# Expert stage: half-width products held in PSUM, head pairs and candidate sums added on GpSimd

## The chip, the cores and the metric

One core of one Trainium2 chip. The metric is the device time of one launch in microseconds, the median of several runs.

## What is computed

The reference passes 16 x 512 rows of 256 numbers through six stages. Stages 1 and 3 are the same expert feed-forward (the change is in these two alone); the others are a dilated attention, two channel mixes and an attention across the batch. The expert part, cut:

```python
q = einsum('btd,ed->bte', h, W_q)                 # 4 heads, two halves each
sx, ix = top_k(sim[0], 8); sy, iy = top_k(sim[1], 8)
all_scores = sx[..., :, None] + sy[..., None, :]   # 64 candidates a head
scores, pk = top_k(all_scores, 8)
indices = take_along_axis(ix * 64 + iy, pk)        # clamped to 1024 experts by the lookup
w = silu(einsum(h, down_embed[indices]) * softmax(scores))
out = dense_mlp(h) + einsum(w, up_embed[indices])
```

## The kernel before

`expert_ffn` works on 256 rows a step: V = 2 tiles (v = 0, 1) of 128 rows. Each of its two stages has 32 steps, unrolled by four. It gathers nothing. For every row it computes the products of h with all 1024 experts (`dots`, into the two banks of `p_dot`), and for each of 4 heads a grid of all 1024 scores (GpSimd, `scores`, one 128x1024 addition a head). ScalarE turns the grid into exponentials (`exps`). VectorE finds the eighth best score of each head and makes the dense weights in two passes a head: `mask` (L648) writes (grid >= threshold) * p_dot to `q` in SBUF, `weigh` (L658) multiplies it in place by 1/z and by the grid. ScalarE applies silu to the whole of `q[v]` (128x4096, L536) and adds the share of the experts beyond 1023 to the last column (`tail`, `clamped`). TensorE transposes `q` in 128x128 blocks and sums the four heads as it does (`turn_w`, L436: 16 matmuls against the identity a call, 4 calls a step), ScalarE copies the transposed weights out (`turned`, L525), and TensorE multiplies them by `eup` (`experts`, L452) on top of the dense part (`dense`, L447).

The thresholds come from VectorE: `sides` takes the 8 best of each side by 12 MAX8 instructions, adds all pairs of them (`cand`, L604), takes the best of those by 8 MAX8 (L610, L611) and negates the best one (`negm`, L616). `listed` (VectorE) subtracts the maximum (`tm`, L621), `listed` (ScalarE) takes the exponential of it (`te`, L511), and `tails` (VectorE) makes z, 1/z (`rz`) and the share of the clamped experts (L627 to L636).

Every engine has its own instruction queue in a fixed order, written out in one function `step(t)` each; engines wait for each other by semaphores (`Track.mark`, `Track.wait`). In step t, VectorE selects for t and finds thresholds for t + 1, GpSimd makes the grids of t + 1, and TensorE finishes tile 1 of t - 1, then tile 0 of t. `p_dot` is single: `dots` for the next tile waits for the last mask of the tile before (mark "tail" of `d_mask`). Two instructions on one engine that depend on each other wait on a semaphore too. PSUM has 8 banks, all used: `p_dot` 2, `p_wT` 2, `p_sim`, `p_hid`, `p_y` 2. `norm.scale` (L195, called by `normed`), `front` (L174, L178) and `root` (GpSimd, L185, L187) are the layer norm of later steps.

Of the kernel before, what the change touches and what calls it, by code (L numbers as in the profile page):

```python
# [219 lines left out]
def expert_ffn(nc, name, src, dst, w):  # L220

    with ExitStack() as ctx:
# [62 lines left out]
        tops, tm, te = (m.sbuf(k, V, HEADS, 2 * TOP) for k in ("tops", "tm", "te"))  # L285
# [19 lines left out]
        d_top = m.track("d_top", *(f"{k}{v}" for v in range(V) for k in ("maxes", "cand", "best", "negm")), "tm")  # L305
        a_te = m.track("a_te")
        d_tail = m.track("d_tail", "z", "seen", "rz", "part", "tail")
        g_grid = m.track("g_grid", "0", "1")
        a_exp = m.track("a_exp", "0", "1")
        t_dot = m.track("t_dot", "0", "1")  # L310
        d_mask = m.track("d_mask", *(f"{v}{k}" for v in range(V) for k in (*range(HEADS), "tail")))
        d_mul = m.track("d_mul", "0", "1")
        a_silu = m.track("a_silu", *(f"{k}{v}" for v in range(V) for k in ("q", "tail", "clamped")))
# [11 lines left out]
        with nc.Block() as block:  # L325
# [25 lines left out]
            def _(pool):  # L351
                def scores(t, v):
                    a_sim.wait(pool, t, str(v))
                    if (t - 1).exists():
                        d_mul.wait(pool, t - 1, str(v))
                    sx = sim[:, v, 0:HEADS * KEYS].rearrange("p (h k) -> p h k", h=HEADS)[:, :, 0:XROWS]
                    sy = sim[:, v, HEADS * KEYS:].rearrange("p (h k) -> p h k", h=HEADS)
                    for hd in range(HEADS):
                        last = pool.tensor_tensor(  # L359
                            grid[v][:, hd, :].rearrange("p (i j) -> p i j", i=XROWS),  # L360
                            sx[:, hd, :].unsqueeze(2).to_broadcast([P, XROWS, KEYS]),
                            sy[:, hd, :].unsqueeze(1).to_broadcast([P, XROWS, KEYS]), ALU.add)
                    g_grid.mark(last, str(v))
# [3 lines left out]
                scores(first, 0)  # L367
                scores(first, 1)
                norm.root(pool, first + 2)

                def step(t):
                    if (t + 1).exists(last=count):
                        scores(t + 1, 0)
                        scores(t + 1, 1)
                    if (t + 3).exists(last=count):
                        norm.root(pool, t + 3)
                turns(pool, count, unroll, step)

            @block.tensor
            def _(pe):  # L380
# [47 lines left out]
                def turn_w(t, v, k):  # L428
                    a_silu.wait(pe, t, f"clamped{v}" if k else f"q{v}")
                    if v:  # L430
                        a_wT.wait(pe, t, f"0{k}")
                    elif (t - 1).exists():
                        a_wT.wait(pe, t - 1, f"1{k}")
                    for e in range(HALF):
                        for hd in range(HEADS):
                            last = pe.matmul(p_wT[k][:, e, :], q[v][:, hd, (k * HALF + e) * P:(k * HALF + e + 1) * P],  # L436
                                             ident[:], is_transpose=True, start=hd == 0, stop=hd == HEADS - 1)
                    t_wT.mark(last, f"{v}{k}")

                def dense(t, v):  # L440

                    if v == 0:
                        a_hid.wait(pe, t, "3")
                    if (t - 1).exists():
                        d_out.wait(pe, t - 1, str(v))
                    for e in range(EC):
                        pe.matmul(p_y[v][:], hs[t.step % 2][:, e, v * P:(v + 1) * P], wdn[:, e, :], start=e == 0, stop=False)  # L447

                def experts(t, v):
                    a_wT.wait(pe, t, f"{v}1")  # L450
                    for e in range(EC):
                        last = pe.matmul(p_y[v][:], wT[v][:, e, :], eup[:, e, :], start=False, stop=e == EC - 1)  # L452
                    t_out.mark(last, str(v))
# [1423 lines left out]
```

How the kernel before makes its waits and increments, by code:

```python
    def wait(self, engine, turn, name=None, alone=False):  # L59
        at = self.marks.index(name) + 1 if name else len(self.marks)
        n = len(self.marks) * self.inc
        engine.wait_ge(self.sem, turn.times(n, at * self.inc))
        if alone:
            engine.nop(nofuse=True)
# [59 lines left out]
    def sync(self, sp):  # L125
        sp.wait_ge(self.s_zero, self.STAGES)
        for n, (src, hi, lo, heads) in enumerate(self.loads):
            if n >= self.STAGES:
                sp.wait_ge(self.s_lo, n - self.STAGES + 1)
            raw = self.raw(n)
            if heads:
                raw = raw.rearrange("p (h s) -> p h s", s=heads[1])[:, :, 0:heads[0]]
                src = src.rearrange("p (h d) -> p h d", d=heads[0])
            sp.dma_start(raw, src).then_inc(self.s_ld[n % self.STAGES], 16)
# [1 line left out]
    def scalar(self, act):  # L136
        for n, (src, hi, lo, heads) in enumerate(self.loads):
            act.wait_ge(self.s_ld[n % self.STAGES], 16 * (n // self.STAGES + 1))
            act.copy(hi, self.raw(n)).then_inc(self.s_hi, 1)
# [1 line left out]
    def vector(self, dve):  # L141
        for k in range(self.STAGES):
            dve.memset(self.stage[k][:], 0.0).then_inc(self.s_zero, 1)
        for n, (src, hi, lo, heads) in enumerate(self.loads):
            dve.wait_ge(self.s_ld[n % self.STAGES], 16 * (n // self.STAGES + 1))
            dve.wait_ge(self.s_hi, n + 1)
            dve.tensor_tensor(lo, self.raw(n), hi.bitcast(F32), ALU.subtract).then_inc(self.s_lo, 1)
```

## Time and profile before

| | us |
|---|---|
| median of 3 runs | 4485.29 |
| lowest, highest | 4482.9, 4485.95 |
| the profiled execution | 4483.73 |
| its span, from first to last instruction | 4481.9 |
| first expert stage, in the span | about 20 to 1205 |
| second expert stage | about 2436 to 3623 |

In the page the busy shares are PE 91%, VectorE 80%, ScalarE 62%, GpSimd 30%. Busy shares are an average over six stages, so what matters here are views of the expert stages alone. Start-to-start times of instructions on one engine are shorter than their durations, because the end of one overlaps the start of the next.

### The profile page before, as it was taken

Reading aid. Unit: us, or ns where it says so; the run is one execution under the profiler, and the core shown is the slowest. Engines: PE = TensorE matmul, PEld = TensorE weight load, DVE = VectorE, ACT = ScalarE, POOL = GpSimd, SP = SyncE. Lnnn points to the kernel's source line nnn. Section 1 sums busy time; section 2 is a strip of 40 time slices with the busy share of each in tenths; the row PEclk is TensorE's granted clock in tenths of the full one; section 3 lists DMA queues with packets and bytes.
Section 4 is the critical chain, followed back from the end, with each engine's and each line's share of the span. In section 5 each row is a group of like instructions: output and inputs, shape, how many; then the busy total and the mean of one; then the engine's idle time right before and its main releaser. Section 6 shows DMA issues by size and latency. Waiting matters only on the chain. (4 is left out here: it accounts for less than half of the span.)

```text
span 4481.9 us, 87959 instructions
## 1 busy us (share of the span) xinstructions
PE 4096.4 (91%) x31208; PEld 3540.6 (79%) x31208; DVE 3574.9 (80%) x7869; ACT 2769.0 (62%) x6709; POOL 1331.1 (30%) x914
## 2 busy tenths in 40 slices
PE   6999999999779999999995999999999979787879
PEld 5988888888667777777774888888888867686756
DVE  7999999999657777777775999999999958445667
ACT  4777767667468887888883776766777723221123
POOL 3544444444221111111101444444444401011200
PEclk9999999999889999999997999999999989898989
DMA  1000000000100000000001000000000012358332
GB/s 59 15 16 15 16 15 15 15 19 14 33 17 11 21 11 21 12 21 21 12 11 64 10 15 16 16 15 20 16 16 15 10 60 89 140 196 246 104 96 76
DMA packets 175295, 180.47 MB, mean 40 GB/s; under 512 B 9552, under 2 KB 167536, under 8 KB 174832
## 3 DMA queue, kind: packets, MB, share of 16 engines
q1 hardware_dynamic: 174832, 174.40, 12.4%
q8 instruction: 278, 4.55, 0.4%
q14 instruction: 185, 1.52, 0.1%
HBM read 98.87 MB, written 75.50 MB: 39 GB/s over the span
## 5 line engine op out<-in xcount | busy, mean ns | idle before, releaser
L359 POOL TENSOR_TENSOR f_grid<-f_sim 128x1024 f32<-128x1024 f32 x512 | 1023.4, 2028 | 1182.2 <-DVE f_q L658 1174.0
L1277 ACT ACTIVATE a_ex<-a_p_s,a_mneg 128x128 f32<-128x128 f32 x2048 | 718.5, 403 | 211.4 <-DVE a_mneg L1322 211.4
L648 DVE SCALAR_TENSOR_TENSOR f_q<-f_grid,f_te,f_p_dot 128x1024 f32<-128x1024 f32 x512 | 620.8, 1273 | 133.4 <-ACT f_grid L517 101.0
L658 DVE SCALAR_TENSOR_TENSOR f_q<-f_q,f_rz,f_grid 128x1024 f32<-128x1024 f32 x512 | 622.5, 1276 | 0.0
L517 ACT ACTIVATE f_grid<-f_grid,f_negm 128x1024 f32<-128x1024 f32 x512 | 545.5, 1138 | 0.0
L1277 ACT ACTIVATION_READ_ACCUMULATOR a_ex<-a_p_s,a_mneg 128x1 f32 x2048 | 498.0, 243 | 0.0
L436 PE MATMUL f_p_wT<-f_ident,f_q 128*128 128x128 f32 x4096 | 480.1, 273 | 4.2 <-ACT f_q L536 4.1
L536 ACT ACTIVATE f_q<-f_q 128x4096 f32<-128x4096 f32 x128 | 464.4, 3628 | 20.9 <-DVE f_q L658 20.0
L436 PEld LDWEIGHTS f_p_wT<-f_ident,f_q 128*128 128x128 f32 x4096 | 457.4, 141 | 20.0 <-ACT f_q L536 4.5
L447 PE MATMUL f_p_y<-f_wdn,f_hs 128*128 128x256 f32 x2048 | 462.8, 379 | 1.4 <-ACT f_hs L531 1.4
L452 PE MATMUL f_p_y<-f_eup,f_wT 128*128 128x256 f32 x2048 | 462.8, 379 | 0.0
L447 PEld LDWEIGHTS f_p_y<-f_wdn,f_hs 128*128 128x128 f32 x2048 | 383.4, 190 | 54.0 <-ACT f_hs L531 1.8
L452 PEld LDWEIGHTS f_p_y<-f_eup,f_wT 128*128 128x128 f32 x2048 | 384.1, 190 | 49.9
L1328 DVE COPY a_exT<-a_p_s 128x512 f32<-128x512 f32 x384 | 264.7, 690 | 181.1 <-PE a_p_s L1147 174.8
L525 ACT COPY f_wT<-f_p_wT 128x512 f32<-128x512 f32 x256 | 143.0, 583 | 370.7 <-PE f_p_wT L436 370.7
L1322 DVE TENSOR_REDUCE a_mneg<-a_p_s 128x4 f32<-128x512 f32 x512 | 343.4, 671 | 11.5 <-PE a_p_s L1136 9.0
L531 ACT ACTIVATE f_hs<-f_p_hid 128x512 f32<-128x512 f32 x256 | 152.2, 594 | 252.2 <-PE f_p_hid L106 252.2
L1147 PE MATMUL a_p_s<-a_ident,a_ex 128*128 128x128 f32 x1536 | 244.7, 282 | 37.4 <-ACT a_ex L1277 37.2
L1147 PEld LDWEIGHTS a_p_s<-a_ident,a_ex 128*128 128x128 f32 x1536 | 166.5, 141 | 102.9 <-ACT a_ex L1277 86.3
L1061 POOL TENSOR_TENSOR a_xb<-a_xt,a_bos 128x256 f32<-128x256 f32 x64 | 44.8, 732 | 490.2 <-DVE a_yt L1360 488.8
L1136 PE MATMUL a_p_s<-a_kT,a_qz 32*128 32x128 f32 x4096 | 151.6, 284 | 37.0 <-DVE a_exT L1328 19.8
L1136 PEld LDWEIGHTS a_p_s<-a_kT,a_qz 32*128 32x128 f32 x4096 | 128.2, 187 | 55.6 <-issue 36.8
(368 smaller groups left out, 9486.6 us busy)
## 6 DMA issues: line engine op xcount, KB each, us to landing
x_f<-f_yt SPq DMA_DIRECT2D x64, 256.0 KB, 2.2
f_xt<-x SPq DMA_DIRECT2D x32, 256.0 KB, 2.8
a_xt<-x_f SPq DMA_DIRECT2D x16, 512.0 KB, 4.2
x_a<-a_yt SPq DMA_DIRECT2D x16, 512.0 KB, 2.9
f_xt<-x_a SPq DMA_DIRECT2D x32, 256.0 KB, 2.8
c_xt<-x_f SPq DMA_DIRECT2D x16, 512.0 KB, 4.6
x_c<-c_yt SPq DMA_DIRECT2D x16, 512.0 KB, 3.1
b1p_xt<-x_c SPq DMA_DIRECT2D x16, 512.0 KB, 4.2
```

What stands on the lines that cost most here:

```text
L359: last = pool.tensor_tensor(grid[v][:, hd, :].rearrange("p (i j) -> p i j", i=XROWS), sx[:, hd, :].unsqueeze(2).to_broadcast([P, XROWS, KE ...
L436: last = pe.matmul(p_wT[k][:, e, :], q[v][:, hd, (k * HALF + e) * P:(k * HALF + e + 1) * P], ident[:], is_transpose=True, start=hd == 0, s ...
L447: pe.matmul(p_y[v][:], hs[t.step % 2][:, e, v * P:(v + 1) * P], wdn[:, e, :], start=e == 0, stop=False)
L452: last = pe.matmul(p_y[v][:], wT[v][:, e, :], eup[:, e, :], start=False, stop=e == EC - 1)
L517: last = act.activation(grid[v][:, hd, :], grid[v][:, hd, :], ACT.Exp, bias=negm[:, v, hd:hd + 1])
L536: a_silu.mark(act.activation(q[v][:], q[v][:], ACT.Silu), f"q{v}")
L648: d_mask.mark(dve.scalar_tensor_tensor(out=q[v][:, hd, :], in0=grid[v][:, hd, :], scalar=te[:, v, hd, TOP - 1:TOP], in1=p_dot[:], op0=ALU. ...
L658: last = dve.scalar_tensor_tensor(out=q[v][:, hd, :], in0=q[v][:, hd, :], scalar=rz[:, v, hd:hd + 1], in1=grid[v][:, hd, :], op0=ALU.mult, ...
L1136: mm = pe.matmul(p_s[i][:, 2 * c + e, :], qz[br][lanes, c, e, j * P:(j + 1) * P], kT[br][lanes, c, j * P:(j + 1) * P], start=True, stop=True)
L1147: last = pe.transpose(p_e[i][:, n, :], ex[t.step % 2][:, i, n, :], ident[:])
L1277: last = act.activation(ex[t.step % 2][:, i, n, :], p_s[i][:, n, :], ACT.Exp, bias=mneg[:, i, n:n + 1], accum_out=z[t.step % 2][:, i, n:n ...
L1322: d_max.mark(dve.tensor_reduce(mneg[:, i, :], p_s[i][:], AX.X, ALU.max, negate=True), str(i))
```

## The change

- Two PSUM banks, `p_u[0]` and `p_u[1]`, hold the masked products. `mask` and `weigh` are cut in halves of 512 experts: 8 + 8 instructions of 128x512 for each tile in place of 4 + 4 of 128x1024. For each head there are two masks to PSUM, then two weighs from PSUM and the grid to `q`.
- The banks come from `p_wT` (one in place of two) and `p_y` (both tiles in one bank), which adds waits: every `turn_w` waits for the copy of the one before, `dense(t, 1)` for `output(t, 0)`, `dense(t, 0)` for `output(t - 1, 1)`.
- GpSimd gets the candidate sums (`pairs`, 128x512), two additions of head pairs for each tile (`summed`, 128x1024, q0 + q1 and q2 + q3 after silu), and a product for the clamped experts (`tails`). `turn_w` then transposes two sums in place of four heads: 8 matmuls a call.
- The grid, its exponentials, mask and weigh are marked and awaited by head. Silu works on two halves of two heads.
- `tm` is gone; ScalarE takes `te` by 8 activations of 128x16 with `negm` as bias. VectorE's five tail instructions become z, rz and 8 small `tensor_scalar` (`seen`).
- The orders on VectorE, GpSimd, ScalarE and TensorE are rewritten: on VectorE the output, `seen`, `maxes`, `best` and `normed` stand between the heads of `select`; on TensorE `dots(t, 1)` stands after `dense(t - 1, 1)` and half of `experts`.

```diff
-        p_wT = [m.psum(f"p_wT{k}", HALF, P) for k in range(2)]
-        p_sim, p_hid = m.psum("p_sim", 512), m.psum("p_hid", 512)
-        p_y = [m.psum(f"p_y{v}", D) for v in range(V)]
+        p_u = [m.psum(f"p_u{e}", 512) for e in range(2)]
+        p_wT, p_sim, p_hid = m.psum("p_wT", HALF, P), m.psum("p_sim", 512), m.psum("p_hid", 512)
+        p_y = m.psum("p_y", V, D)
...
+                def pairs(t, v):
+                    d_top.wait(pool, t, f"maxes{v}")
+                    g_cand.mark(pool.tensor_tensor(cand[:, v]..., tx[:, v]..., ty[:, v]..., ALU.add), str(v))
...
+                def summed(t, v, k):
+                    a_silu.wait(pool, t, f"clamped{v}" if k else f"front{v}")
+                    g_pair.mark(pool.tensor_tensor(q[v][:, 2 * k, :], q[v][:, 2 * k, :], q[v][:, 2 * k + 1, :], ALU.add),
+                                f"{v}{k}")
...
                 def step(t):      # GpSimd
-                    if (t + 1).exists(last=count):
-                        scores(t + 1, 0)
-                        scores(t + 1, 1)
-                    if (t + 3).exists(last=count):
-                        norm.root(pool, t + 3)
+                    tails(t)
+                    if after:
+                        pairs(t + 1, 0)
+                        scores(t + 1, 0, (0, 1))
+                    summed(t, 0, 0)
+                    summed(t, 0, 1)
+                    if after:
+                        pairs(t + 1, 1)
+                        scores(t + 1, 0, (2, 3))
+                    summed(t, 1, 0)
+                    if after:
+                        scores(t + 1, 1, (0,))
+                    summed(t, 1, 1)
+                    if (t + 3).exists(last=count):
+                        norm.root(pool, t + 3)
+                    if after:
+                        scores(t + 1, 1, (1, 2, 3))
...
                 def step(t):      # TensorE
                     if before:
                         turn_w(t - 1, 1, 0)
-                        turn_w(t - 1, 1, 1)
                     if after:
                         similar(t + 1, 1)
-                    dots(t, 1)
                     hidden(t, 0)
                     if before:
+                        turn_w(t - 1, 1, 1)
                         dense(t - 1, 1)
+                        experts(t - 1, 1, 0)
+                    dots(t, 1)
+                    if before:
+                        experts(t - 1, 1, 1)
                     hidden(t, 1)
...
                 def listed(t):    # ScalarE
-                    d_top.wait(act, t, "tm")
+                    d_top.wait(act, t, "negm1")
...
-                    a_te.mark(act.activation(te[:], tm[:], ACT.Exp))
+                    for v in range(V):
+                        for hd in range(HEADS):
+                            last = act.activation(te[:, v, hd, :], tops[:, v, hd, :], ACT.Exp, bias=negm[:, v, hd:hd + 1])
...
                 def step(t):      # ScalarE
                     if after:
                         similar(t + 1, 0)
-                    exps(t, 1)
+                    exps(t, 1, (0, 1))
                     if before:
                         turned(t - 1, 1, 0)
                         turned(t - 1, 1, 1)
+                    exps(t, 1, (2, 3))
                     if after:
                         similar(t + 1, 1)
                     hidden(t, 0)
                     weights(t, 0)
...
+                def mask(t, v, hd, e):
+                    d_mask.mark(dve.scalar_tensor_tensor(out=p_u[e][:], in0=grid[v][:, hd, half_e],
+                                                         scalar=te[:, v, hd, TOP - 1:TOP], in1=p_dot[:, half_e],
+                                                         op0=ALU.is_ge, op1=ALU.mult), f"{v}{hd}{e}")
+                def weigh(t, v, hd, e):
+                    d_mul.mark(dve.scalar_tensor_tensor(out=q[v][:, hd, half_e], in0=p_u[e][:],
+                                                        scalar=rz[:, v, hd:hd + 1], in1=grid[v][:, hd, half_e],
+                                                        op0=ALU.mult, op1=ALU.mult), f"{v}{hd}{e}")
...
                 def step(t):      # VectorE
+                    for v in range(V):
+                        select(t, v, (0,))
+                        if before:
+                            output(t - 1, v)
+                        if v == 0:
+                            seen(t)
+                        select(t, v, (1,))
+                        if after:
+                            maxes(t + 1, v)
+                        select(t, v, (2, 3))
+                        if after:
+                            best(t + 1, v)
+                        if v == 0 and later:
+                            normed(t + 2)
                     if later:
                         turned(t + 2)
                     if (t + 3).exists(last=count):
                         front(t + 3)
                     if after:
-                        tails(t + 1)
+                        inverse(t + 1)
```

## Rows read from the trace of the kernel before

**Rows 1.** Busy time PE, PEld, DVE, ACT, POOL (instructions); granted clock; DMA.

```profile
200.00:900.00 700.00, 690.29 (x4210) 618.47 (x4210) 646.93 (x1498) 488.38 (x580) 328.83 (x194) 1.00 0.05 16
```

**Rows 2.** Waits from 200 to 900 us: total, times, longest.

```profile
POOL f_grid L359 <- DVE f_q L658: 374.1, 39, 13.2
```

**Rows 3.** Timeline of PE within one step: start, length, instructions.

```profile
508.13 3.61 PE L447 MATMUL f_p_y<-f_wdn,f_hs 128*128 128x256 f32 x16
...
516.42 3.66 PE L436 MATMUL f_p_wT<-f_ident,f_q 128*128 128x128 f32 x32
519.84 0.47 PE L104 MATMUL f_p_sim<-f_wsl,f_hT2h 128*128 128x512 f32 x1
...
521.65 0.50 PE L104 MATMUL f_p_dot<-f_wdownl,f_hT1h 128*128 128x512 f32 x1 [0.18 <-DVE f_u L651]
...
524.55 0.28 PE L104 MATMUL f_p_hid<-f_hT1l,f_wuph 128*128 128x256 f32 x1
...
525.96 3.62 PE L447 MATMUL f_p_y<-f_wdn,f_hs 128*128 128x256 f32 x16
```

**Rows 4.** Timeline of VectorE over one step.

```profile
516.64 4.85 DVE L648 SCALAR_TENSOR_TENSOR f_q<-f_grid,f_te,f_p_dot 128x1024 f32<-128x1024 f32 x4 [1.92 <-ACT f_grid L517]
...
536.52 0.41 DVE L667 SCALAR_TENSOR_TENSOR f_yt<-f_p_y,f_xt 128x256 f32<-128x256 f32 x1
536.86 4.86 DVE L658 SCALAR_TENSOR_TENSOR f_q<-f_q,f_rz,f_grid 128x1024 f32<-128x1024 f32 x4
541.64 0.16 DVE L599 MAX8 f_tx<-f_sim 128x8 f32<-128x16 f32 x1
...
543.01 1.30 DVE L604 TENSOR_TENSOR f_cand<-f_tx,f_ty 128x512 f32<-128x512 f32 x1
544.42 0.29 DVE L610 MAX8 f_tops<-f_cand 128x8 f32<-128x128 f32 x1
...
545.83 0.27 DVE L616 TENSOR_SCALAR f_negm<-f_tops 128x4 f32<-128x4 f32 x1
...
548.16 1.83 DVE L628 TENSOR_TENSOR f_tail<-f_te 128x64 f32<-128x64 f32 x1
...
552.43 4.85 DVE L648 SCALAR_TENSOR_TENSOR f_q<-f_grid,f_te,f_p_dot 128x1024 f32<-128x1024 f32 x4 [1.92 <-ACT f_grid L517]
```

**Rows 5.** Timeline of ScalarE, end of the same step.

```profile
541.78 3.64 ACT L536 ACTIVATE f_q<-f_q 128x4096 f32<-128x4096 f32 x1
...
545.65 0.29 ACT L539 ACTIVATE f_q<-f_q,f_clamped 128x1 f32<-128x1 f32 x1
546.39 1.28 ACT L511 ACT_TABLE_LOAD   x1 [0.44 <-DVE f_tm L621]
547.68 0.31 ACT L511 ACTIVATE f_te<-f_tm 128x128 f32<-128x128 f32 x1
547.90 4.25 ACT L517 ACTIVATE f_grid<-f_grid,f_negm 128x1024 f32<-128x1024 f32 x4
```

**Rows 6.** Timeline of GpSimd, same step.

```profile
541.86 8.05 POOL L359 TENSOR_TENSOR f_grid<-f_sim 128x1024 f32<-128x1024 f32 x4 [6.75 <-DVE f_q L658]
```

**Rows 7.** VectorE in the first stage's start, while GpSimd adds grids.

```profile
41.05 0.27 DVE L616 TENSOR_SCALAR f_negm<-f_tops 128x4 f32<-128x4 f32 x1
41.24 0.28 DVE L621 TENSOR_TENSOR f_tm<-f_tops 128x128 f32<-128x128 f32 x1
41.44 3.89 DVE L195 TENSOR_SCALAR f_h<-f_xt,f_mv,f_rstd 128x256 f32<-128x256 f32 x2
```

**Rows 8.** Durations by line: ns min/median/max, first and last start.

```profile
L195 DVE TENSOR_SCALAR f_h<-f_xt,f_mv,f_rstd x128: 404/408/1985, 25.9 to 3514.9; 128x256 f32<-128x256 f32 x128
...
L1061 POOL TENSOR_TENSOR a_xb<-a_xt,a_bos x64: 717/733/746, 1252.4 to 2329.9; 128x256 f32<-128x256 f32 x64
```

**Rows 9.** VectorE timeline in a later stage, 128x512 products.

```profile
3639.43 1.41 DVE L878 SCALAR_TENSOR_TENSOR c_xk<-c_diff,c_mu,c_hT 128x512 f32<-128x512 f32 x2
```

**Rows 10.** PE in the attention stage: busy time (instructions), granted clock.

```profile
1300.00:1400.00 100.00, 91.32 (x1190) 1.00 0.02 7
```

More of the change, by code:

```diff
@@ L365, in _, with tails @@
+                def tails(t):
+                    d_rz.wait(pool, t, "seen")
+                    g_tail.mark(pool.tensor_tensor(tail[:], tail[:], te[:, :, :, TOP:], ALU.mult))
                 norm.root(pool, first)
                 norm.root(pool, first + 1)
-                scores(first, 0)
-                scores(first, 1)
+                pairs(first, 0)
+                scores(first, 0, range(HEADS))
+                pairs(first, 1)
                 norm.root(pool, first + 2)
+                scores(first, 1, range(HEADS))
@@ L434, in turn_w @@
                     for e in range(HALF):
[L435 to L437 removed]
+                        for hd in (0, 2):
+                            last = pe.matmul(p_wT[:, e, :], q[v][:, hd, (k * HALF + e) * P:(k * HALF + e + 1) * P],
+                                             ident[:], is_transpose=True, start=hd == 0, stop=hd == 2)
@@ L449, in experts @@
[L449 to L453, printed above, removed]
+                        pe.matmul(p_y[:, v, :], hs[t.step % 2][:, e, v * P:(v + 1) * P], wdn[:, e, :], start=e == 0, stop=False)
+                def experts(t, v, k):
+                    a_wT.wait(pe, t, f"{v}{k}")
+                    for e in range(k * HALF, (k + 1) * HALF):
+                        last = pe.matmul(p_y[:, v, :], wT[v][:, e, :], eup[:, e, :], start=False, stop=e == EC - 1)
+                    if k:
+                        t_out.mark(last, str(v))
@@ L491, in _ @@
                 dense(end, 1)
-                experts(end, 1)
+                for k in range(2):
+                    experts(end, 1, k)
             @block.scalar
@@ L546, in _ @@
                 listed(first)
-                exps(first, 0)
+                exps(first, 0, range(HEADS))
                 def step(t):
@@ L655, in weigh, with inverse @@
-                def weigh(t, v):
-                    for hd in range(HEADS):
-                        d_mask.wait(dve, t, f"{v}{hd}")
-                        last = dve.scalar_tensor_tensor(out=q[v][:, hd, :], in0=q[v][:, hd, :],
-                                                        scalar=rz[:, v, hd:hd + 1], in1=grid[v][:, hd, :],
-                                                        op0=ALU.mult, op1=ALU.mult)
-                    d_mul.mark(last, str(v))
+                def inverse(t):
+                    a_te.wait(dve, t)
+                    d_rz.mark(dve.tensor_reduce(z[:], te[:, :, :, 0:TOP], AX.X, ALU.add), "z")
+                    d_rz.wait(dve, t, "z")
+                    d_rz.mark(dve.reciprocal(rz[:], z[:]), "rz")
@@ L674, in _ @@
                 turned(first)
-                sides(first, 0)
-                sides(first, 1)
-                listed(first)
+                maxes(first, 0)
+                best(first, 0)
+                maxes(first, 1)
+                best(first, 1)
                 normed(first + 1)
@@ L680, in _ @@
                 turned(first + 1)
-                tails(first)
+                inverse(first)
                 def step(t):
                     before, after, later = (t - 1).exists(), (t + 1).exists(last=count), (t + 2).exists(last=count)
-                    mask(t, 0)
-                    if later:
-                        normed(t + 2)
-                    weigh(t, 0)
-                    if after:
-                        sides(t + 1, 0)
-                    if before:
-                        output(t - 1, 0)
-                    mask(t, 1)
-                    if before:
-                        output(t - 1, 1)
-                    weigh(t, 1)
-                    if after:
-                        sides(t + 1, 1)
-                        listed(t + 1)
+                    for v in range(V):
+                        select(t, v, (0,))
+                        if before:
+                            output(t - 1, v)
+                        if v == 0:
+                            seen(t)
[7 more added lines that the diff above has]
+                            normed(t + 2)
                     if later:
```

184 lines of the change are left out of this document (97 added, 87 removed).

## Prediction

> **What bounds the kernel now.** I read first the busy times of a stretch inside the first expert stage, then the waits, then each engine's timeline over one step. TensorE is busy 690 of 700 us at the full 2.4 GHz (clock 1.00) [rows 1], so its queue is nearly full. One step, from one first mask of tile 0 to the next, takes 552.43 - 516.64 = 35.79 us [rows 4]. VectorE is close behind: within this step it idles only 1.92 us, for the first exponentials of the next step [rows 4]. Besides, some of its instructions are longer than their work: `cand` 1.30 us for 512 elements, a 64-element comparison (L628) 1.83 us [rows 4]. Both run while GpSimd adds grids (541.86 to 549.91 [rows 6]), and L628 ends at 549.99, just as the last of these does. At the stage's start the two L195 take 3.89 us, where the median of one is 0.408 [rows 7, 8]: each waited for about a whole addition of GpSimd (8.05/4 = 2.0 us [rows 6]). So VectorE and GpSimd shut each other out in some instructions. `negm` and `tm` together got through at one boundary [rows 7]. The masks don't suffer: 4.85 us for four, beside GpSimd or not [rows 4]. GpSimd's own wait is for VectorE's weighs, 374 us in 39 times [rows 2]; it is idle over half of the time.
>
> The Trainium skill, "SBUF — State Buffer", section "SBUF: two separate sides", states this as an exclusive lock between GpSimd and VectorE instructions with two SBUF inputs or in a 2-port mode. The rows agree. The new weighs have one input in PSUM and would by that rule go free; `seen` and `normed` would not, which is the fourth term below.
>
> **The change part by part, for one step.** TensorE: 32 transposes took 3.42 us from their start to the next start (519.84 - 516.42), 0.107 each [rows 3]. Half of 64 go, or 3.42 us; TensorE needs 35.79 - 3.42 = 32.4 or less. VectorE: a half product costs 0.66 start to start (two take 1.41, each 0.75 alone [rows 9]); a full one 1.195 ((541.64 - 536.86)/4 [rows 4]). So 32 halves take 21.1 against 19.1 for 16: +2.0. No row has an output in PSUM; I take the row of SBUF. The low bound is 0.60 (1.195/2), the high one 0.72. Off VectorE go `cand` twice (2 x 1.4, 543.01 to 544.42), `tm` (0.2) and most of the 2.4 us of tails [rows 4, 7]; 8 short `seen` come, 0.08 each if free (0.65).
>
> Let T be the end of the last weigh of a step (before: 541.7) and M the first mask of the next (552.43): 10.7 us [rows 4]. **First term, T to M after.** The silu of the last two heads is half of 3.64, about 1.95. The sums behind it end 0.52 later (541.78 + 3.64 = 545.42 to 545.94), at T + 2.55. The table load follows, 1.28, to T + 3.85 [rows 5]. `te` is now 8 activations with bias; the nearest is L539, 0.29 less an overlap of 0.1, about 0.2 each, 1.7 in all against 0.31 [rows 5]. So te is there at T + 5.55 and the first head's exponential (four take 4.25, one with its overlap 1.14) at T + 6.7: M = T + 6.75. The bound from below is 1.0 for the eight (T + 6.05), from above 2.3 (T + 7.35).
>
> **Second term, VectorE through a step.** Tile 0: four heads of 2.64, output 0.34, seen 0.65, maxes 1.37 (541.64 to 543.01), best and negm 1.7 (544.42 to 546.01 and two waits), u8 0.1, normed 0.65 [rows 4, 8]: 15.4, or T + 22.15 if nothing is in the way. Tile 1: 10.56 + 0.34 + 1.37 + 0.1 and the last end: 12.45. T to T: 34.6.
>
> **Third term, the dots of tile 1.** They now stand behind a chain through ScalarE and TensorE. The four exponentials end at T + 9.8 (5.55 + 4.25 [rows 5]), the copy of `p_sim` at T + 10.3. Then TensorE does similar (1.6), hidden (1.4, 524.55 to 525.96), `turn_w` (0.9), dense (3.45), half of the experts (1.75) and dots (2.9, 521.65 to 524.55, and 0.2 until VectorE may start) [rows 3]: T + 22.7. A step then takes 22.7 + 12.45 = 35.15, 0.64 less than before.
>
> **Fourth term, what GpSimd's new work does to VectorE.** The nearest row to `summed` is L1061, 0.733 for 256 elements of two dense inputs [rows 8]; with 0.2 fixed, 1024 take 2.35 us. The grid's 1.9 is the low bound, 0.733 x 4 = 2.9 the high one. GpSimd has then 4 x 2.35 + 8 x 1.9 + 2 x 1.05 + 1.3 = 28 us a step, and few holes. `seen` falls at T + 9.7 into the grids of tile 1 (about T + 7 to T + 12.7): it waits for a boundary, about 1.15, and I let all eight pass there. ScalarE reaches the first silu of tile 0 by exponentials, copies, table load and hidden at T + 19.3, and ends it at T + 21.2; `summed(t, 0, 0)` runs T + 21.3 to 23.6. `negm` comes at T + 22.4, waits till 23.6, and with normed VectorE comes to tile 1 at T + 24.4. A step: 24.4 + 12.45 = 36.85, that is +1.06. Over the 62 steps that follow another, +66 us; the first steps add about 3, since the first grid now stands behind `pairs`. 4483.7 + 69 = 4552.7 by the profiled execution, which lies 1.6 under the median: forecast 4553 us. `summed` at 1.9 would give 36.4, at 2.9 37.4.
>
> The Trainium skill, "GPSIMD Engine Reference", section 3.1, measures 4497 ns for an addition of 2048; by it `summed` would take about 2.25 us and the step 0.1 less. No row here has that operation.
>
> Costed at nothing: the waits for the single `p_wT` and `p_y` bank. The copies (0.6) lie under hidden; `output(t, 0)` comes at M + 3, five us before dense(t - 1, 1) wants its bank. If that cover went, each copy would put 0.6 on the third term, which has 1.7 to spare in the forecast. `pairs` ends 3 us before `best` wants it. TensorE will idle some 4.5 us a step, the longest gap before similar(t + 1, 1) (T + 7.5 to T + 10.3). In the attention stage it is 91% busy and its clock holds 1.00 [rows 10], so I take no loss.
>
> **The rivals.** (a) The lock hardly bites: `seen` and `normed` fall into holes. Then the step is 35.15, and with halves at 0.60 34.4: 4435 to 4447 us, faster. For it: most of VectorE's work (masks, MAX8) is untouched beside GpSimd. Against it: L628 and L195, and a GpSimd that is twice as busy. It decides where the fourth term is under 1.0 (tile 1 reached before T + 23.3). (b) Each of the normed pair and of `seen` waits for a whole addition, as the two L195 did [rows 7]: one more addition before tile 1 (clamped at T + 23.6, so to T + 26), 38.8 a step, 4483.7 + 62 x 3.0 = 4670 us. (c) TensorE stays the bound and VectorE keeps up: -3.42 x 64 = -219, 4265 us. Against it: the second term alone asks 34.6. (d) The terms cancel, within 9 us. (e) TensorE's clock falls in the new gap: similar and hidden at 1.2 GHz cost 3 us more, 1.3 beyond the slack, about 4630 us.
>
> **How the numbers follow.** The forecast's case (fourth term 1.0 to 2.2 over the third, 4490 to 4600 us) has 0.42; (a) 0.28; (b) and (e) 0.18; (c) 0.03; (d) 0.09. The likeliest alone has 4495 to 4600. Bounds of the half product move it by -2.0 (0.60; both tiles 0.06 x 32) to +2.0 us a step, in part hidden in tile 0. For 8 in 10 the range takes in most of (a) and the lower half of (b): 4425 to 4640. 0.2% is 9 us, about what a measurement of this kernel can tell from no change: faster 0.31, same 0.09, slower 0.60.
>
> **What would show it.** Right: a step of 36 to 37.5 between first masks; halves near 0.66; L195 or `negm` stretched to 1 to 2 us, `seen` stretched; TensorE busy 86 to 89% in the stage with idle before p_sim and p_dot; GpSimd 75% busy. Wrong: `normed` at 0.41 throughout (then (a)); `te` far from 1.7; the dots of tile 1 released by VectorE rather than late from TensorE's own queue; a half product far from 0.66 because its output is in PSUM.

## The result and the profile after

The changed kernel takes 4628.41 us (median of 4 runs, 4627.35 to 4629.51) against 4484.48 us for the one before (4 runs), a ratio of 1.032 [1.030, 1.034]: 144 us slower. The forecast was 4553. The span of its profiled execution is 4627.7 us.

The same stretch of 200 to 900 us, in the columns of [rows 1]:

```profile
200.00:900.00 700.00, 620.46 (x3349) 536.69 (x3348) 630.75 (x1726) 496.40 (x717) 507.44 (x313) 0.96 0.05 14
```

TensorE fell from 690 busy us to 620 and GpSimd rose from 329 to 507. VectorE looks unchanged (647 to 631) although it does less in the same time: part of what is called busy is waiting inside an instruction. The mean granted clock fell from 1.00 to 0.96. The waits of the stretch (total, times, longest) name no large new wait:

```profile
POOL f_cand L358 <- DVE f_ty L653: 153.8, 36, 5.7
...
PE f_p_dot L104 <- DVE f_u L719: 35.5, 18, 2.7
...
DVE f_p_u L697 <- ACT f_grid L566: 20.9, 19, 3.0
...
DVE f_p_u L697 <- PE f_p_dot L106: 7.0, 8, 1.0
```

VectorE waits for dots 7 us and for exponentials 21 us, and GpSimd now waits for VectorE's `maxes` where it waited for the weighs before [rows 2]. The loss shows only in a timeline. VectorE over one step, `maxes` and `best` left out:

```profile
539.32 1.40 DVE L705 SCALAR_TENSOR_TENSOR f_q<-f_p_u,f_rz,f_grid 128x512 f32<-128x512 f32 x2
...
542.03 0.59 DVE L668 TENSOR_SCALAR f_negm<-f_tops 128x4 f32<-128x4 f32 x1
...
547.28 1.42 DVE L697 SCALAR_TENSOR_TENSOR f_p_u<-f_grid,f_te,f_p_dot 128x512 f32<-128x512 f32 x2 [0.58 <-ACT f_grid L566]
548.60 1.41 DVE L705 SCALAR_TENSOR_TENSOR f_q<-f_p_u,f_rz,f_grid 128x512 f32<-128x512 f32 x2
...
550.25 4.29 DVE L682 TENSOR_SCALAR f_tail<-f_te,f_rz 128x8 f32<-128x8 f32 x8
554.46 1.40 DVE L697 SCALAR_TENSOR_TENSOR f_p_u<-f_grid,f_te,f_p_dot 128x512 f32<-128x512 f32 x2
...
562.29 0.18 DVE L719 TENSOR_TENSOR f_u<-f_tail,f_p_dot 128x32 f32<-128x32 f32 x1
...
565.11 0.69 DVE L668 TENSOR_SCALAR f_negm<-f_tops 128x4 f32<-128x4 f32 x1
565.72 0.72 DVE L195 TENSOR_SCALAR f_h<-f_xt,f_mv,f_rstd 128x256 f32<-128x256 f32 x2
566.36 1.40 DVE L697 SCALAR_TENSOR_TENSOR f_p_u<-f_grid,f_te,f_p_dot 128x512 f32<-128x512 f32 x2
...
577.25 1.40 DVE L705 SCALAR_TENSOR_TENSOR f_q<-f_p_u,f_rz,f_grid 128x512 f32<-128x512 f32 x2
```

and GpSimd beside it:

```profile
547.73 5.62 POOL L371 TENSOR_TENSOR f_grid<-f_sim 128x1024 f32<-128x1024 f32 x3
554.62 0.32 POOL L385 TENSOR_TENSOR f_tail<-f_tail,f_te 128x64 f32<-128x64 f32 x1 [1.27 <-DVE f_tail L682]
...
563.36 2.41 POOL L379 TENSOR_TENSOR f_q<-f_q 128x1024 f32<-128x1024 f32 x1
566.35 2.39 POOL L379 TENSOR_TENSOR f_q<-f_q 128x1024 f32<-128x1024 f32 x1 [0.58 <-ACT f_q L590]
```

Read the two side by side. The last weigh ends at 540.72 (T) and the next one at 578.65: a step of 37.93 us, against 35.79 [rows 4]. Eight `seen` on 64 elements in all take 4.29 us. GpSimd's three grids end at about 549.6, 551.5 and 553.35. `seen` begins in the second and ends at 554.54, 1.19 us after the third. One at a time, the first two of the eight are:

```profile
550.25 1.27 DVE L682 TENSOR_SCALAR f_tail<-f_te,f_rz 128x8 f32<-128x8 f32 x1
...
551.44 1.95 DVE L682 TENSOR_SCALAR f_tail<-f_te,f_rz 128x8 f32<-128x8 f32 x1
```

The first ends at 551.52, with the second grid. The next waits through the whole third grid and ends at 553.38. The other six take 0.28 each, 0.2 from start to start. So one `seen` gets through at 551.5, and seven are left. `negm` (565.11 to 565.80) ends with the addition of GpSimd (565.77), 0.5 late. The two L195 here fall where GpSimd itself waits 0.58, and go free.

Durations by line (ns min, median, max) tell the two kinds of instruction apart:

```profile
L682 DVE TENSOR_SCALAR f_tail<-f_te,f_rz x512: 275/280/2049, 53.2 to 3730.9; 128x8 f32<-128x8 f32 x171
...
L697 DVE SCALAR_TENSOR_TENSOR f_p_u<-f_grid,f_te,f_p_dot x1024: 725/744/758, 50.6 to 3750.9; 128x512 f32<-128x512 f32 x171
...
L379 POOL TENSOR_TENSOR f_q<-f_q x256: 2343/2390/2426, 65.6 to 3755.7; 128x1024 f32<-128x1024 f32 x128
```

A `seen` can last 2.05 us for 0.28. Of 1024 masks, with one input in PSUM, none is stretched. None of this kernel's 512 grid additions is either (1.893 to 1.932 us), nor are the sums of pairs: here it is VectorE that pays.

From one z to the next, four steps in a row take 37.92, 37.86, 38.66 and 38.95 us, a mean of 38.35. The mean before is 36.12 (from first mask to first mask 35.79, 35.79, 37.2, 35.70; one step of four holds the turn of the loop, in both kernels). From its first z to its last, the first expert stage takes 1110.3 us before the change and 1185.8 after it, the second one 1112.3 and 1184.9. That is 148 us more, so the whole of the measured 144 lies in the two expert stages.

Not all of it is the ordinary step. In most steps, as in the one above, tile 1 starts as soon as VectorE gets to it; in others it waits for its dots. One of these, TensorE and then VectorE:

```profile
638.33 0.50 PE L104 MATMUL f_p_dot<-f_wdownl,f_hT3h 128*128 128x512 f32 x1 [2.51 <-DVE f_u L719]
...
640.81 0.63 PE L106 MATMUL f_p_dot<-f_wdownh,f_hT3h 128*128 128x512 f32 x1
...
642.93 1.41 DVE L697 SCALAR_TENSOR_TENSOR f_p_u<-f_grid,f_te,f_p_dot 128x512 f32<-128x512 f32 x2 [0.80 <-PE f_p_dot L106]
```

TensorE had been idle for 2.51 us. The first of its twelve dots start 0.23 apart, those after 640 start 0.43 apart, the level of 1.2 GHz (the granted clock from 639.9 to 642.5 is 0.50), and VectorE waits 0.80 for them. Over both stages tile 1 waits 28.6 us for its dots, in 27 of 64 steps. In 25 of these, 22.8 us in all, the dots take 3.6 us or more from the first start to the last, where they take 2.67 at full rate; the other two are the last step of each stage.

### The profile page after: what moved, and what is told of

The parts are those of the page before. It is cut to its first block and busy times, and to the rows that moved or that the text cites. A ratio compares the mean times of both kernels' runs of the same rounds, so it can differ in the third digit from the quotient of the medians.

```text
span 4627.7 us, 88219 instructions
## 1 busy us (share of the span) xinstructions
PE 3999.5 (86%) x29160; PEld 3389.9 (73%) x29160; DVE 3662.8 (79%) x9021; ACT 2881.3 (62%) x7285; POOL 2023.5 (44%) x1362
## 5 line engine op out<-in xcount | busy, mean ns | idle before, releaser
L371 POOL TENSOR_TENSOR f_grid<-f_sim 128x1024 f32<-128x1024 f32 x512 | 963.9, 1904 | 0.0
L697 DVE SCALAR_TENSOR_TENSOR f_p_u<-f_grid,f_te,f_p_dot 128x512 f32<-128x512 f32 x1024 | 717.5, 744 | 92.0 <-ACT f_grid L566 63.4
L705 DVE SCALAR_TENSOR_TENSOR f_q<-f_p_u,f_rz,f_grid 128x512 f32<-128x512 f32 x1024 | 716.5, 739 | 0.0
L379 POOL TENSOR_TENSOR f_q<-f_q 128x1024 f32<-128x1024 f32 x256 | 611.6, 2389 | 76.2 <-ACT f_q L590 40.9
L492 PE MATMUL f_p_y<-f_eup,f_wT 128*128 128x256 f32 x2048 | 476.2, 381 | 0.0
L358 POOL TENSOR_TENSOR f_cand<-f_tx,f_ty 128x512 f32<-128x512 f32 x128 | 136.9, 1070 | 539.1 <-DVE f_ty L653 539.1
L587 ACT ACTIVATE f_q<-f_q 128x2048 f32<-128x2048 f32 x128 | 245.3, 1916 | 197.6 <-DVE f_q L705 197.6
L1212 PE MATMUL a_p_s<-a_ident,a_ex 128*128 128x128 f32 x1536 | 245.2, 283 | 38.8 <-ACT a_ex L1342 38.7
L474 PE MATMUL f_p_wT<-f_ident,f_q 128*128 128x128 f32 x2048 | 267.8, 274 | 10.9 <-ACT f_wT L573 8.7
L474 PEld LDWEIGHTS f_p_wT<-f_ident,f_q 128*128 128x128 f32 x2048 | 233.5, 141 | 21.4 <-ACT f_wT L573 9.5
L682 DVE TENSOR_SCALAR f_tail<-f_te,f_rz 128x8 f32<-128x8 f32 x512 | 246.6, 557 | 0.0
```

The costliest lines, as they stand in the source:

```text
L371: g_grid.mark(pool.tensor_tensor(grid[v][:, hd, :].rearrange("p (i j) -> p i j", i=XROWS), sx[:, hd, :].unsqueeze(2).to_broadcast([P, XROW ...
L379: g_pair.mark(pool.tensor_tensor(q[v][:, 2 * k, :], q[v][:, 2 * k, :], q[v][:, 2 * k + 1, :], ALU.add), f"{v}{k}")
L474: last = pe.matmul(p_wT[:, e, :], q[v][:, hd, (k * HALF + e) * P:(k * HALF + e + 1) * P], ident[:], is_transpose=True, start=hd == 0, stop ...
L492: last = pe.matmul(p_y[:, v, :], wT[v][:, e, :], eup[:, e, :], start=False, stop=e == EC - 1)
L682: last = dve.tensor_scalar(tail[:, v, hd, :], te[:, v, hd, TOP:], te[:, v, hd, TOP - 1:TOP], rz[:, v, hd:hd + 1], ALU.is_ge, ALU.mult)
L697: d_mask.mark(dve.scalar_tensor_tensor(out=p_u[e][:], in0=grid[v][:, hd, half_e], scalar=te[:, v, hd, TOP - 1:TOP], in1=p_dot[:, half_e], ...
```

## The experiments

The theory (A): TensorE's saving is real but no longer the bound, and the added time is what GpSimd's additions take from VectorE's short SBUF instructions. The rivals: their own cost, the longer chain through `te`, or TensorE late with the dots. All kernels start from the changed one, and every ratio is to the kernel before. The diffs are cut, those of runs 2, 4 and 5 abridged. Where a recorded expectation names a kernel, e1_seen_later is run 1, e7_out_of_the_way run 6 and e9_te_one_too run 8.

**1. `seen` moved behind the maxes of tile 0.**

```diff
                         if before:
                             output(t - 1, v)
-                        if v == 0:
-                            seen(t)
                         select(t, v, (1,))
                         if after:
                             maxes(t + 1, v)
+                        if v == 0:
+                            seen(t)
```

> The eight short instructions of seen are moved behind the maxima of tile 0, where GpSimd has no addition to do. Theory A (they cost 4.2 us a step where they stand, because they are shut out by two of GpSimd's additions, and only 1.5 us by themselves): seen takes 1.5 to 1.6 us, the step between first masks falls from 37.9 to about 35.3 us, 4628 - 62 x 2.6 = 4467 us (4450 to 4495). Rival B (the dots of tile 1, late through ScalarE's and TensorE's queues, set the start of tile 1): seen gets shorter but the first mask of tile 1 waits for p_dot instead, and the time stays within 15 us of 4628.

Measured: 4583.51 us, 1.021 [1.020, 1.023]. `seen` is free, but only 45 us are won where 161 were expected. VectorE and GpSimd later in a step:

```profile
542.37 1.63 DVE L682 TENSOR_SCALAR f_tail<-f_te,f_rz 128x8 f32<-128x8 f32 x8
...
550.68 1.76 DVE L668 TENSOR_SCALAR f_negm<-f_tops 128x4 f32<-128x4 f32 x1
552.36 2.87 DVE L195 TENSOR_SCALAR f_h<-f_xt,f_mv,f_rstd 128x256 f32<-128x256 f32 x2
...
550.03 4.72 POOL L379 TENSOR_TENSOR f_q<-f_q 128x1024 f32<-128x1024 f32 x2 [0.88 <-ACT f_q L585]
```

`seen` takes 1.63 us when nothing is in its way, 0.2 each. With VectorE earlier, `negm` and the L195 now fall into the two additions of head pairs. `negm` ends at 552.44, where the first addition does (550.03 + 4.72/2 = 552.39). The L195 end at 555.23, 0.48 after the second (554.75). The first of the two by itself:

```profile
552.36 2.55 DVE L195 TENSOR_SCALAR f_h<-f_xt,f_mv,f_rstd 128x256 f32<-128x256 f32 x1
```

It is shut out by the whole second addition; the other takes 0.40. So `negm` alone got through between the two additions, as one `seen` did above. This happens in about half of the steps (38.5 us each). In the others `negm` and both L195 are free, VectorE waits 1.26 us for dots that TensorE starts late, and the step is 36.16: that is rival B's mechanism, once VectorE is through.

**2. `seen` as one comparison of 128x64 behind the maxes**, its two products on GpSimd:

```diff
-  for v, hd: tensor_scalar(tail[:, v, hd, :], te[..., TOP:], te[..., TOP-1:TOP], rz[:, v, hd], is_ge, mult)
+  d_rz.mark(dve.tensor_tensor(tail[:], te[..., TOP:], te[..., TOP - 1:TOP].to_broadcast(...), ALU.is_ge), "seen")
```

> As before, and seen is one comparison of 128x64 on VectorE; the two products for the clamped experts are on GpSimd. Theory A: another 1.3 us of VectorE goes, but then the dots of tile 1 end last (TensorE was ready for them 2.5 us before VectorE let it): the first mask of tile 1 waits for p_dot some 0.5 to 1 us, step about 34.9, 4440 us (4420 to 4465). Rival B: no change against 4628. Rival C (the half products and the longer way to the thresholds are the loss, the lock is incidental): at best 1 us a step, 4560.

Measured: 4486.82 us (4472 to 4495), 1.000 [0.999, 1.001]. Steps of 34.61 us, 1.2 shorter than before the change, stand beside ones of 38.9 (from last weigh to last weigh) that hold the turn of the loop, where `negm` takes 1.2 and the second L195 2.47, and some of 36.16 behind these, in which the dots are late. Better than run 1 by 97 us, 47 short of the expectation, and in part for the same reason: `negm` and L195. Two things change here at once: `seen` is out of the additions' way, as in run 1, and its own cost falls from 1.6 us to 0.2.

**3. Only the head pairs undone**: TensorE transposes all four heads again, GpSimd adds none.

```diff
-                    summed(t, 0, 0)
-                    summed(t, 0, 1)
...
-                        for hd in (0, 2):
+                        for hd in range(HEADS):
```

> Only the head pairs are undone: TensorE transposes and sums four heads again (32 more matmuls a step, 3.4 us), GpSimd has no summed. If TensorE were still the bound, the step would grow by 3.4 us: 4628 + 219 = 4847 us. Theory A: TensorE has some 5 us of idle time in a step and takes them there, while GpSimd, 9.6 us a step lighter, gets its grids done earlier, so that seen meets one addition rather than two: step about 36.2, 4520 us (4490 to 4640).

Measured: 4500.62 us, 1.003 [1.002, 1.004]. The stretch of 200 to 900 us:

```profile
200.00:900.00 700.00, 690.14 (x4185) 619.43 (x4183) 615.75 (x1849) 522.46 (x756) 353.05 (x251) 1.00 0.05 15
```

TensorE is the bound again at 690 busy us and steps of 35.76, as before the change, and eight `seen` take 1.64. Undoing the pairs returns 128 of the 144 us. Without them GpSimd's three grids end at 560.64 and `seen` begins at 560.44, so it meets only their end. In the changed kernel, then, the saved transposes buy nothing, and the additions of pairs cost at least these 128 us, above all by putting the grids into VectorE's way. All the other edits together, the half products in PSUM among them, cost 16 us net beside a TensorE that is full.

**4. `seen` in its place, as two instructions of 128x64.**

```diff
-  eight tensor_scalar 128x8 (is_ge, mult)
+  tail = te[TOP:] >= te[TOP-1]      # one instruction, marked "flag"
+  tail = tail * rz                  # one instruction, waits for "flag"
```

> seen in its place, but as two instructions of 128x64 (comparison, product) instead of eight of 128x8. Theory A, each such instruction waits for the end of an addition and the next addition gets in between: first 1.2, then 1.9, and 0.2 itself, 3.3 us against 4.2: 4628 - 62 x 0.9 = 4572 us (4560 to 4590). Rival D (the eight cost by their number, about 0.5 each): 0.4 to 0.5 us, step 34.5 to 35.3, 4420 to 4465 us.

Measured: 4632.3 us, 1.033 [1.031, 1.034].

```profile
551.79 1.33 DVE L680 TENSOR_TENSOR f_tail<-f_te 128x64 f32<-128x64 f32 x1
553.16 1.83 DVE L684 TENSOR_TENSOR f_tail<-f_tail,f_rz 128x64 f32<-128x64 f32 x1
```

To the next mask the two take 3.12 us, 1.1 less than the eight, and each is stretched (run 6 has one such at 0.22). That is theory A's size for `seen`, and rival D's 0.4 to 0.5 falls. But the time doesn't fall, a miss of 60 us: two steps of four take 36.75, 1.1 less than in the changed kernel, and in the other two tile 1 is then kept by `negm` and L195, as in run 1 (40.05, the first L195 2.54).

**5. `te` by one subtraction on VectorE and one activation**, as before the change.

```diff
-  for v, hd: activation(te[:, v, hd, :], tops[:, v, hd, :], Exp, bias=negm[:, v, hd])
+  a_te.mark(act.activation(te[:], tm[:], ACT.Exp))     # tm = tops - max on VectorE, at the end of select
```

> The changed kernel with te as it was: one subtraction on VectorE and one activation of 128x128 instead of eight of 128x16. The way from the last weigh to the first mask falls from 6.6 to about 5.2 us. Rival C (the longer way to the thresholds is a loss of its own): the step falls by the same 1.4 us, 4628 - 62 x 1.3 = 4547 us. Theory A (seen can't end before GpSimd's last grid addition, which follows the end of the step before and not the masks): seen only waits longer, 5 to 5.6 us, and the time falls by less than 25 us: 4603 to 4635 us.

Measured: 4665.77 us, 1.040 [1.038, 1.041]: slower still. The chain through `te` is shorter in about half of the steps, where the first mask comes at T + 5.2 in place of T + 6.6. The rest of the step gives it back and more:

```profile
560.12 5.63 DVE L684 TENSOR_SCALAR f_tail<-f_te,f_rz 128x8 f32<-128x8 f32 x8
...
579.43 1.42 DVE L699 SCALAR_TENSOR_TENSOR f_p_u<-f_grid,f_te,f_p_dot 128x512 f32<-128x512 f32 x2 [1.91 <-PE f_p_dot L106]
...
593.57 2.07 DVE L669 TENSOR_TENSOR f_tm<-f_tops 128x128 f32<-128x128 f32 x1
```

`seen` meets GpSimd's run of grids 1.4 earlier and ends no earlier. In the other steps `tm` is shut out in its turn (2.07 for 0.28), and the first mask is back at T + 6.7. The third line is new. TensorE over the same dots:

```profile
573.73 0.79 PE L104 MATMUL f_p_dot<-f_wdownl,f_hT1h 128*128 128x512 f32 x1 [3.85 <-DVE f_u L721]
574.32 0.63 PE L105 MATMUL f_p_dot<-f_wdownh,f_hT1l 128*128 128x512 f32 x1
...
579.02 2.22 PE L492 MATMUL f_p_y<-f_eup,f_wT 128*128 128x256 f32 x8
```

The dots of tile 1 wait for VectorE's last mask of tile 0 (its `u`). Here TensorE had been idle for 3.85 us, the granted clock from 570 to 580 was 0.66, and the dots took 5.29 us (573.73 to 579.02), where in the changed kernel's first step above they took 2.9 (562.52 to 565.43). So a late VectorE makes TensorE idle, then slow, and waits for it: the shut-out costs twice. The changed kernel pays this too, 0.80 in its second step above; in this run it is 68.8 us in 48 steps.

**6. All three out of the way**: run 2, and besides the two L195 behind the maxes of tile 0 and `negm` for both tiles as one instruction at the step's end.

```diff
                             maxes(t + 1, v)
+                        if v == 0:
+                            if later:
+                                normed(t + 2)
+                            seen(t)
...
-                        if v == 0 and later:
-                            normed(t + 2)
+                    if after:
+                        negated(t + 1)
```

> Beyond the single comparison, normed moves to where GpSimd waits for VectorE (behind the maxima of tile 0, ahead of the comparison), and negm is one instruction at the end of the step. So nothing that GpSimd can shut out stands between the heads. Theory A: no step meets an addition any more (L195 0.40 throughout), the first mask of tile 1 waits for p_dot in every step, each is 34.6 us as the free steps of the run before, and the mean with the loop's turn 35.2: 4478 - 64 x 0.7 = 4430 us (4415 to 4450), 1.2% under the kernel before. If the shut-out is not what costs: no change against 4487.

Measured: 4441.55 us, 0.991 [0.989, 0.993], 187 us under the changed kernel. One step:

```profile
552.18 0.72 DVE L195 TENSOR_SCALAR f_h<-f_xt,f_mv,f_rstd 128x256 f32<-128x256 f32 x2
552.82 0.22 DVE L686 TENSOR_TENSOR f_tail<-f_te 128x64 f32<-128x64 f32 x1
...
561.06 1.41 DVE L701 SCALAR_TENSOR_TENSOR f_p_u<-f_grid,f_te,f_p_dot 128x512 f32<-128x512 f32 x2 [1.37 <-PE f_p_dot L106]
```

Nothing between the heads is stretched (`negm`, at the step's end, takes 0.59 while VectorE would wait for `te` anyway), and ordinary steps take 34.62. Tile 1 begins at 561.06, which is T + 22.3 (T = 538.75), and what it waits for is dots that started late in TensorE's own queue (557.70, directly behind half of the experts, without a wait). How much of the 187 us is the shut-out, and how much the 1.4 us a step that one comparison costs less than eight `seen`, is not separated: no run has eight `seen` with all three out of the way.

**7. The dots of tile 1 moved ahead of that half of the experts**, on top of run 6.

```diff
                         dense(t - 1, 1)
-                        experts(t - 1, 1, 0)
                     dots(t, 1)
                     if before:
+                        experts(t - 1, 1, 0)
                         experts(t - 1, 1, 1)
```

> In addition TensorE does the dots of tile 1 ahead of the first half of the experts of the tile before, which brings them 1.73 us forward. If the third term of the prediction (dots late by TensorE's own order) is what is left, VectorE is ready at about 21.2 us after the last weigh and the step falls to some 33.4 to 33.8 us, 34.2 in the mean: about 4365 us (4340 to 4400). If VectorE or the output of the tile before binds instead: within 15 us of the run before.

Measured: 4441.09 us, 0.990 [0.988, 0.992]: nothing gained, a miss of 76 us. In this run the dots wait for the last mask of tile 0 in all 20 steps (26 us), which they did in 4 of 20 before. Without the half of the experts they can start only 0.6 us sooner, as that mask then bounds them, and tile 1 starts at T + 21.67 in place of T + 22.31. The output behind the moved experts now waits for `p_y` (11.7 us in 20 times, 0.6 each). The gain is spent. `negm` at the step's end grows from 0.59 to 0.92, but the next first mask stays at T + 6.57.

**8. `te` by one activation once more**, on top of run 7.

> In addition te is one activation again, of one subtraction on VectorE. With nothing shut out, the 1.3 us between the last weigh and the first mask are now on the path: step 32.4 to 32.8, 4290 us (4265 to 4350). If dots through ScalarE's queue bind, they come 1.3 us earlier too, so the same. Then TensorE, 32 us of work a step, is nearly full again and may hold it at 32.3.

Measured: 4405.03 us, 0.982 [0.980, 0.983], the fastest kernel of the study. It missed the expectation by 115 us. In a step:

```profile
539.35 1.51 DVE L195 TENSOR_SCALAR f_h<-f_xt,f_mv,f_rstd 128x256 f32<-128x256 f32 x2
...
548.37 1.41 DVE L700 SCALAR_TENSOR_TENSOR f_p_u<-f_grid,f_te,f_p_dot 128x512 f32<-128x512 f32 x2 [0.72 <-PE f_p_dot L106]
```

The first mask comes 1.35 earlier (T + 5.22 against T + 6.57), but L195 now touches a grid (1.51 in place of 0.72), and the step shrinks by 0.57, to 34.05. The same edit cost 37 us in run 5 and gains 36 here: what differs is that `seen` and the `negm` of tile 0 no longer stand where the time won is lost again.

**9. Run 8 with the head pairs undone.**

> e9_te_one_too with the head pairs undone (TensorE transposes all four heads again, GpSimd adds none). In the changed kernel this undoing took 128 us off. Theory: that was the price of GpSimd's additions shutting out VectorE, and where seen, normed and negm are out of the way it is paid no more, so here the undoing only gives TensorE its 32 transposes back, 3.42 us a step. TensorE then sets the step again at 35.3 to 35.8 us against a mean of 34.8 in e9_te_one_too: 4440 to 4480 us. Rival: the head pairs on GpSimd cost VectorE time wherever the short instructions stand; then the undoing gains here too, under 4395 us.

Measured: 4494.86 us, 1.002 [1.001, 1.003]; TensorE busy 690.83 of 700 us, ordinary steps 35.76. The rival falls. The result lies 15 us above the expected range, which left out the turn of the loop (37.1 us in one step of four, from last weigh to last weigh). Undoing the head pairs takes 128 us off the changed kernel and puts 90 us on run 8: they pay only where VectorE is not shut out.

**10. Only L195 and `negm` moved, the eight `seen` left in place.**

> The changed kernel with only normed and negm out of the way (normed behind the maxes of tile 0, negm one instruction at the end of the step); seen stays in its place as eight instructions. Theory A: each step pays once, at whichever short instruction meets GpSimd first; in the changed kernel that is seen (4.2 us), while normed is not blocked there, so moving normed and negm alone gives at most 0.4 us a step: 4600 to 4630 us, seen still 4 us or more. Rival: normed and negm carry a share of their own in the changed kernel (they were the difference between e1_seen_later and e7_out_of_the_way, 142 us); then this falls to 4490 to 4560 us.

Measured: 4746.0 us, 1.058 [1.057, 1.060], outside both theories. `seen` still takes 4.29 us, as A had it. VectorE around the start of tile 1, and then TensorE:

```profile
627.05 0.17 DVE L722 TENSOR_TENSOR f_u<-f_tail,f_p_dot 128x32 f32<-128x32 f32 x1
...
632.10 1.42 DVE L700 SCALAR_TENSOR_TENSOR f_p_u<-f_grid,f_te,f_p_dot 128x512 f32<-128x512 f32 x2 [2.27 <-PE f_p_dot L106]
...
627.27 0.50 PE L104 MATMUL f_p_dot<-f_wdownl,f_hT2h 128*128 128x512 f32 x1 [3.93 <-DVE f_u L722]
```

Moved ahead of the last masks of tile 0, the L195 delay its last one: from the first mask to `u` 16.40 us (571.84 to 588.24 in the step before) against 15.01 in the changed kernel. There `negm` and the L195 ran after that mask, largely while TensorE made the dots, and cost at most 0.6: from `u` to the first mask of tile 1 the changed kernel takes 4.07 us, and this one 3.50 where TensorE's clock holds. Besides, TensorE idles 3.93 us here and then makes most of the dots at 0.43 a matmul in place of 0.23 (granted clock 0.88 from 620 to 630), so `u` to the first mask takes 5.05 us; in the step before, at clock 1.00, 3.50. Over both stages tile 1 waits 136.5 us for its dots, against 28.6 in the changed kernel. Nearly the whole of the 118 us lies in the expert stages (117 more from first z to last). Theory A had the cost of `seen` right and missed what the move does to the last mask of tile 0. Run 6 has the same move and gains by it, as without `seen` ahead VectorE is at its last mask 11.58 us after the first one (545.32 to 556.90), before TensorE is ready for the dots.

## Why the prediction was right or wrong

The sign and the mechanism were right and the result lies in the range, 12 us below its upper end, but the loss was forecast at 69 us and is 144. The step that failed is the fourth term: it let all eight `seen` through at one boundary of GpSimd's additions, and they took 4.2 us in place of 1.8. Beside it, TensorE's clock was costed at nothing ("I take no loss"), and the waits that it brings come to 22.8 us.

- **TensorE** (32.4 us a step or less, 86 to 89% busy): right, 620 of 700 is 89%. Rival (c) would have needed it as the bound. Run 3, with four heads to transpose again, shows it as such.
- **First term** (M = T + 6.75): measured T + 6.56. `te` took the forecast 1.7 and was there at T + 5.5.
- **Second term**: the half product takes 0.66 (547.28 to 548.60 for two), so its output in PSUM costs no more than in SBUF. The masks and maxes of tile 0 were 0.23 faster than forecast.
- **Third term** (dots of tile 1 at T + 22.7, from TensorE's own queue): in the changed kernel it is not seen, as VectorE's last mask releases the dots in 18 steps of 19. That was named as a sign of error. The durations listed for this term add up to T + 22.5, not T + 22.7, which changes nothing in the forecast, as the fourth term ends later. The term itself is right where VectorE is let through: run 6 has T + 22.3, from TensorE's queue.
- **Fourth term**, mis-sized. "It waits for a boundary, about 1.15, and I let all eight pass there" gave `seen` 1.8 us; it took 4.21 to the next mask (550.25 to 554.46). About 0.9 of the difference is its own cost (0.2 each, run 1, where 0.08 was taken); the other 1.5 is that the second `seen` waits for a whole further addition (1.66 beyond its own 0.2), less 0.16 by which the first wait was shorter than forecast. What spoke for letting them pass was `negm` and `tm`, which did get through together before [rows 7]; there the addition that followed, at 41.26, took 2.01 us in place of 1.90. Why `seen` and L195 don't pass in pairs and those two did, no run shows. `negm` and the L195 were given 2.0 and took 1.25, since GpSimd happened to wait. Tile 1 then began at 566.36 = T + 25.64 in place of 24.4: -0.19 (M) + 2.41 (`seen`) - 0.75 - 0.23 = +1.24. With tile 1 0.16 faster the step is 37.93, not 36.85.
- **TensorE's clock**, costed at nothing from the attention stage's 1.00. It falls after the gap before the dots: 22.8 us over both stages, a sixth of the loss. In sum: the ordinary step rose by 2.13 (37.92 - 35.79), 132 us over 62 steps, and with the 28.6 of all waits for dots that is 161; the 148 measured in the stages leaves 13 the other way. Part of this is the turn of the loop, an estimate from single steps: it adds about 1 us to one step of four before (36.8) and 0.1 now (38.03), as `seen` then comes later, meets one addition and takes 2.03.
- **A sign that misled.** "`normed` at 0.41 throughout (then (a))" came true, 0.399 to 0.413 in all 128 L195, and (a) did not hold: the shut-out fell on `seen`, and on `negm` (median 0.59, 0.17 when free).
- **Costed at nothing**: `p_wT` and `p_y`. No run gives them two banks again, so this stays open; run 3 has the single banks, and there they and all other edits but the pairs cost 16 us net.

The Trainium skill, "SBUF — State Buffer", section "SBUF: two separate sides", says that whichever of the two engines starts first has the shared pair "for the whole instruction". The trace agrees: the stretched ones end with an addition of GpSimd (565.80 and 565.77), and 1024 masks with an input in PSUM stay within 725 and 758 ns. It agrees the other way round as well, where VectorE is first (last section).

Of the rivals, (b) came nearest by its mechanism, one whole addition more: it priced this at 38.8 us a step and 4670, and the ordinary steps are 37.93, the mean 38.35. It put the shut-out on both `seen` and the L195; in the changed kernel it is nearly all in `seen`, and moves to `negm` and L195 only as `seen` leaves (runs 1 and 4). (a) describes run 6: 34.62 a step and 4441 us, inside its 4435 to 4447, though with one comparison for eight `seen`. (e) names 4630, two us from the result, and that is luck: it charges the clock to `similar` and `hidden`, where it is covered. TensorE in the first step above, at similar(t + 1, 1):

```profile
550.89 0.79 PE L104 MATMUL f_p_sim<-f_wsl,f_hT2h 128*128 128x512 f32 x1 [2.28 <-ACT f_sim L549]
...
562.52 0.50 PE L104 MATMUL f_p_dot<-f_wdownl,f_hT1h 128*128 128x512 f32 x1 [0.95 <-DVE f_u L719]
```

After a gap of 2.28 us the granted clock of 550 to 560 is 0.83. But TensorE is still ready for the dots 0.95 before VectorE has done the last mask of tile 0, so the slow matmuls are covered there. Where the gap stands before the dots themselves it can be paid, as in the changed kernel's second step above and more often in runs 5 and 10.

## What to carry to other kernels

Before work is given to GpSimd, list the VectorE instructions on the path of the kinds that were shut out here (`tensor_scalar` on SBUF, `tensor_tensor` with both inputs in SBUF; MAX8 and products with an input in PSUM were not), and lay their times over GpSimd's additions: one on the path can cost a whole addition however short it is, the next in a row can be shut out by the next addition, and eight small ones are worse than one (4.2 us in place, 1.6 free; two took 3.1, one 0.2 when free). To move the one that is shut out only passes the wait on to the next such instruction; the order pays once all are out of GpSimd's runs, and here the same change went from 3.2% slower to 0.9% faster by that and a cheaper `seen` (run 6), and to 1.8% with `te` in one activation as well (run 8). And an instruction must not be moved out of the shadow of another engine's work: what it hid behind there, it delays elsewhere (run 10).

## What the runs showed of the hardware

- Either engine can be the one that waits. In the changed kernel GpSimd's additions were always there first: three grids beside the shut-out `seen` took 5.62 us, 1.87 each. In the kernel before, four took 8.05, 2.01 each [rows 6], mainly because one of them came behind a VectorE instruction, `cand`, that was already running (543.01 to 544.31 [rows 4]):

```profile
543.73 2.35 POOL L359 TENSOR_TENSOR f_grid<-f_sim 128x1024 f32<-128x1024 f32 x1
```

A grid alone takes 1.90. Of the 512 grids before, 128 take about 2.35, each of them beside one of the 128 `cand`.

- What was stretched is `tensor_scalar` on SBUF (128x4, 128x8 and 128x256, up to 1.38, 2.05 and, in run 1, 2.58 us) and `tensor_tensor` with two inputs in SBUF (128x64 and 128x128, 1.83 and 2.07). The MAX8, which read SBUF too, stay within 0.15 and 0.30.
- GpSimd's addition of 1024 elements costs 2.39 us with two dense inputs (2343 to 2426 ns in 256) and 1.87 to 1.9 for a grid, whose inputs are repeated; the 512 of `pairs`, of the second kind, 1.07. The forecast 2.35, from 256 dense elements, held.
- TensorE's clock can fall just after it starts again: in run 10, after 3.93 us idle, it began the dots at full rate and was at 0.43 us a matmul, the 1.2 GHz level, from the third to the tenth (628.00 to 630.98). After 2.51 us idle, in the changed kernel, it fell at the sixth (above), and in other steps with the same gap it did not (twelve dots in 2.67 us after 2.52). The changed kernel, with its gaps of 2 to 3 us, has a mean of 0.96 in the stretch; run 3, busy 690 of 700 us, kept 1.00.
